# Two transformer-like acts on one core: no added room behind the reciprocals, and optional work of each act's first stage laid into its first phases

## The reference

```
x = x + squared_attention(norm(x))   # scores squared, causal, divided by their row sums, then @ Wo
x = x + gated_attention(norm(x))     # one key/value head, picked per token by an argmax gate; softmax
x = x + mqa_attention(norm(x))       # one key/value head, softmax, biases, then @ out_w
x = x + gated_attention(norm(x))     # the same weights as layer 2
```

## Time and profile before

| what | value |
|---|---|
| median of 3 runs | 4017.52 us (4014.93 to 4022.45) |
| the profiled execution's own time | 4020.66 us |
| its span in the profile | 4018.9 us |
| PE busy | 3647.1 us, 91% |
| POOL busy | 2982.7 us, 74% |
| DVE busy | 2170.1 us, 54% |
| ACT busy | 1624.3 us, 40% |
| mean granted clock of TensorE | 0.977 |
| first keys burst of the first act | at 94.77 us |
| first keys burst of its second stage | at 307.91 us |
| second act's first keys burst | at 1104.43 us |

### The profile page before, as it was taken

One profiled execution on the slowest core, in us unless ns is written; L12 is line 12 of the kernel. 1 busy time (PEld: TensorE's weight loads), 2 busy tenths in 40 slices (PEclk: granted clock), 3 DMA queues, 4 the chain that ended last, 5 costly groups with the idle time before them and its releaser, 6 DMA issues.

```text
span 4018.9 us, 66697 instructions
## 1 busy us (share of the span) xinstructions
PE 3647.1 (91%) x25570; PEld 1450.4 (36%) x25570; DVE 2170.1 (54%) x5132; ACT 1624.3 (40%) x2433; POOL 2982.7 (74%) x2207
## 2 busy tenths in 40 slices
PE   8899999997989999999888888888998999999976
PEld 5343534432333333333333333333333333333332
DVE  1222323233556766666666656565665666676663
ACT  1554545554043333434444434343332334343343
POOL 3988788896067767777888877787667677776786
PEclk9999999998999999999999999999999999999997
DMA  2000101020110010100101010010101001010011
GB/s 74 27 6 27 38 16 48 6 70 33 45 33 1 32 32 1 64 1 25 40 13 53 6 48 12 30 35 17 48 1 35 30 1 64 1 54 1 1 43 32
DMA packets 63286, 115.02 MB, mean 29 GB/s; under 512 B 8576, under 2 KB 9088, under 8 KB 62976
## 3 DMA queue, kind: packets, MB, share of 16 engines
q1 hardware_dynamic: 62976, 110.75, 8.5%
HBM read 77.17 MB, written 33.55 MB: 28 GB/s over the span
## 4 chain that ended last, share of the span: by engine, by line
PE 54%; DVE 7%; ACT 6%; issue 4%; POOL 3%; DMA 0%; POOLq 0%; SPq 0%; DVEq 0%; ACTq 0%
PE banks L1181 11%; PE banks L1134 11%; PE banks L1166 9%; PE banks L1228 8%; PE banks L1127 7%; ACT probs_soft L870 5%; PE banks L1163 3%; DVE banks L966 3%; PE banks L1327 3%; DVE maxima_soft L961 2%; POOL added_soft L781 2%; PE banks L1195 1%; DVE rest_soft L1085 1%; DVE maxima_soft L966 1%; PE banks L1325 0%
## 5 line engine op out<-in xcount | busy, mean ns | idle before, releaser
L870 ACT ACTIVATE probs_soft<-banks 128x1024 f32<-128x1024 f32 (+1 forms) x960 | 848.4, 936 | 1195.1 <-PE banks L1166 1171.2
L781 POOL TENSOR_TENSOR added_soft<-added_soft,probs_soft 128x512 f32<-128x512 f32 (+1 forms) x380 | 1153.0, 3034 | 21.3 <-POOL added_soft L774 6.4
L966 DVE CUSTOM_DVE_ANT_0 banks<-banks,mask 128x128 f32<-128x128 f32 (+3 forms) x1536 | 701.3, 528 | 516.5 <-PE banks L1181 516.0
L961 DVE TENSOR_REDUCE maxima_soft<-banks 128x2 f32<-128x1024 f32 x384 | 452.6, 1221 | 367.5 <-PE banks L1181 367.4
L1181 PE MATMUL banks<-k_soft,q_soft 32*128 32x512 f32 (+3 forms) x4608 | 499.7, 525 | 77.6 <-ACT probs_soft L870 77.4
L876 ACT ACTIVATE probs_squared<-banks,key_scale_squared 128x512 f32<-128x512 f32 (+3 forms) x768 | 379.7, 590 | 341.5 <-PE banks L1166 337.1
L1127 PE MATMUL banks<-xnT,wide 128*128 128x512 f32 x1024 | 509.9, 620 | 5.0 <-DVE rest_soft L1085 1.9
L1134 PE MATMUL banks<-wide,xnT 128*128 128x512 f32 x1024 | 497.0, 613 | 1.0 <-ACT q_soft L853 1.0
L1166 PE MATMUL banks<-q_soft,k_soft 32*128 32x512 f32 (+3 forms) x4608 | 476.0, 495 | 0.0
L758 POOL TENSOR_SCALAR_AFFINE_SELECT probs_soft<-probs_soft 128x512 f32<-128x512 f32 x384 | 239.4, 637 | 313.8 <-ACT probs_soft L870 308.3
L1228 PE MATMUL banks<-probs_soft,v_soft 128*32 128x512 f32 (+3 forms) x4608 | 438.3, 499 | 20.2 <-ACT q_soft L855 4.8
(11 more groups left out here) (136 smaller groups left out, 4075.7 us busy)
## 6 DMA issues: line engine op xcount, KB each, us to landing
tiles<-out SPq DMA_DIRECT2D x96, 256.0 KB, 2.7
rest_soft<-out SPq DMA_DIRECT2D x96, 256.0 KB, 2.9
out<-rest_soft SPq DMA_DIRECT2D x96, 256.0 KB, 2.1
tiles<-in_x SPq DMA_DIRECT2D x32, 256.0 KB, 2.7
rest_squared<-in_x SPq DMA_DIRECT2D x32, 256.0 KB, 2.8
out<-rest_squared SPq DMA_DIRECT2D x32, 256.0 KB, 2.0
wide<-in_gated_wqkvT SPq DMA_DIRECT2D x3, 1024.0 KB, 7.6
probs_squared<-in_squared_wk SPq DMA_DIRECT2D x1, 1024.0 KB, 5.5
```

Of the source, the lines that this page charges most:

```text
L781: ins = pool.tensor_tensor(sums, sums, slot(ph, n)[:, :, col:col + width], ALU.add)
L870: ins = act.activation(slot(ph, n)[:, 2 * a:2 * a + 2, 0:width], score_pair(e, a)[:, :, 0:width], ACT.Exp, scale=SCALE)
L961: ins = dve.reduce_max(m["maxima"][:, ph % 2, 2 * a:2 * a + 2, t, p], score_pair(e, a)[:, :, col:col + width], AX_X)
L966: ins = dve.tensor_tensor_reduce(scores, scores, k["mask"][:, CHUNK - width:CHUNK], 1.0, MASKED, ALU.add, ALU.max, m["maxima"][:, ph % 2, ...
```

## The change

It has three parts. First, the constant `INVERTED` is gone: the halves that hold a reciprocal (`inv`) no longer get 0.85 more room, so `spread` lays the same optional work of the second act out more evenly. Second, in the first act only the values of the first two head groups and the features (`k2`, `q2`, `ksq`, `kvar`) of group 0 stay in front of the first phase; the features of group 1 (`rest`) become a work list of their own, due 2 halves before the end of phase 0, and the values of the other two groups one that is due 4 halves into phase 2. `since` lets them come from the start. Third, in the second act the second chunk of group 1's queries moves from in front of the `rows` bursts to between them, both key transposes (`kt`) come behind its first chunk, and the last two of the 8 `vall` move from between the `rows` bursts into phase 0, due at its half 6.

```diff
-INVERTED = 0.85
@@ keys_and_values
+        if s == 0:
+            return [("gt", s, 0)], first + [("krep", s, 1), queries[1][0], ("kt", s, 0), ("kt", s, 1)], \
+                [queries[1][1]] + [("vall", s, t) for t in range(NT)]
         first += [queries[1][0], ("krep", s, 1), ("kt", s, 0), queries[1][1], ("kt", s, 1)]
@@ phase
         for event, later in sums_done(kinds[of // NG], of, c):
             at[first + later].append(event)
-            if event[0] == "inv":
-                room[first + later] += INVERTED
@@ since
+    if event[0] == "v2" and event[1] == 0 or event[0] in ("q2", "k2") and event[1] < NG:
+        return 0
@@ plan
-        events += between + first
+        values = [e for e in between + first if e[0] == "v2"]
+        events += [e for e in values if e[2] == 0] + [e for e in first if e[0] != "v2"]
+        behind_first = [(in_pieces(rest, kinds), HALVES - 2), (in_pieces([e for e in values if e[2]], kinds), 2 * HALVES + 4)]
     if soft:
         rows = [("rows", 0, k) for k in range(NRB)]
+        behind_first = [(in_pieces(rest[len(rows) - 2:], kinds), 6)]
+        rest = rest[:len(rows) - 2]
...
-    else:
-        events += rest
...
+        if s == 0:
+            work = work[:1] + behind_first + work[1:]
```

## The result

| | before | after |
|---|---|---|
| median of the runs that were compared | 4018.23 us (4014.93 to 4022.45) | 3956.92 us (3951.94 to 3962.06) |
| ratio, 95% interval | | 0.9847 [0.983, 0.9864] |
| the profiled execution's own time | 4020.66 us | 3959.07 us |
| its span | 4018.9 us | 3957.3 us |

The kernel is 61 us (1.5%) faster.

The account below looks back on a forecast made before the run. PE, busy 91% of the span, bounds the kernel; only its idle time and slow stretches can be won. -18.0 - 2.0 - 10.0 + 2.5 (more rows in PE's list) = -27.5, from the median 4017.52 to 3990 us, range 3968 to 4010.

Parts of the forecast that it names:

- Part 1: First act's start: work moved behind the first keys burst fills PE's idle and slow time, 18.0 us gained.
- The sum's idle part: First act's first phases: 20.5 us of PE idle time goes, less 5 for POOL and 1.3 behind ACT's first squaring.
- The sum's clock part: First act's first phases: about 5.1 us of slow matmuls goes, less 1.3 of slow clock behind remaining waits.
- Part 2: Second act's start: 7.3 us of moved work goes to a stretch with idle time, 2 us gained, bounds -3 and 7.
- Part 3: Second act, no added room behind the reciprocals: net 10 us gained, bounds 25 gained and 45 lost.
- (a): Second act, sixth keys burst: a piece fills PE's 1.03 us wait for masked maxima in 14 of 27 phases, 13 us gained.
- (b): Second act: fewer outputs queue behind DVE's reciprocals, so a quarter of PE's 37 us of bank waits goes, 9 us.
- (c): Second act, bursts behind the reciprocals: PE arrives sooner and waits more for unmasked maxima, 12 us lost.
- Levelling wins more: Rival, chance 0.17: even pieces in the second act also shrink the 159 short waits for the exponential; 3968 us.
- POOL keeps the start: Rival, chance 0.14: first act's removed waits return in phases 1 and 2, gaining only 10 there; 4009 us.
- reciprocals decide: Rival, chance 0.06: in 43 second-act phases a keys burst waits for maxima behind DVE's reciprocals, 44 us lost; 4044 us.
- Slow clock from chopping: Rival, chance 0.03: moved matmuls between short waits run at half clock, costing 29.5 us more; about 4020 us.

Follow-up runs that it names:

- the changed kernel: The kernel before with only the second act's start changed: 4023.75 us, ratio 1.001.
- a step of 0.2 or 0.4 below zero: Room behind reciprocals 0.2 below zero, on the kernel before with only the first act's start changed: 4003.74 us; 0.4 below zero, on the kernel after: 4010.62 us.
- 0.85, 0.4, 0 and -0.2: Added room behind the reciprocals, on the kernel before with only the first act's start changed: 4006.23, 3942.63, 3954.99 and 4003.74 us.

## Why the prediction was off, step by step

**Part 1, the first act's start: the waits were right, the clock was not.** Predicted 18 us, measured 13.7 alone [8.8 to 18.5]. The start of PE in the kernel after:

```profile
64.95 1.14 PE L1171 MATMUL banks<-q_squared,k_squared 32*128 32x512 f32 x8
66.03 5.42 PE L1132 MATMUL banks<-xnT,wide 128*128 128x512 f32 x12
...
175.56 1.99 PE L1293 MATMUL banks<-wide,xnT 128*128 128x256 f32 x8 [1.13 <-ACT sums_squared L860]
...
188.67 1.71 PE L1233 MATMUL banks<-probs_squared,v_squared 128*32 128x512 f32 x16 [2.78 <-POOL probs_squared L763]
```

The keys burst stands at 64.95 (predicted 65.3). Of the two waits of the earlier trace rows the one of 5.48 us for the squares is gone, and the 9.57 us have become 2.78 (predicted 5). The product behind it takes 1.71 instead of 3.21 us, so the clock held there. The 1.3 us behind ACT's late first squaring didn't come: PE goes on at 66.03 without a wait. POOL in the kernel after, against the earlier trace rows:

```profile
72.58 0.64 POOL L763 TENSOR_SCALAR_AFFINE_SELECT probs_squared<-probs_squared 128x512 f32<-128x512 f32 x1 [2.53 <-ACT probs_squared L881]
...
187.88 0.64 POOL L763 TENSOR_SCALAR_AFFINE_SELECT probs_squared<-probs_squared 128x512 f32<-128x512 f32 x1
```

Its first mask stands at 72.58 (predicted 72.8), the mask that releases the product ends at 188.52, 8 us behind the earliest time of 180.6 that the working gave. POOL does pause where PE's list grew longer, as it said; but PE comes to that product at 185.9 and not at 178, so that only 2.78 us of it showed.

The sum's idle part, 20.5 less 5 and 1.3, is 14.2 us, and PE's idle time in this stage did fall by 14.2 (23.0 to 8.8). That the two agree to the tenth is luck: the wait for POOL is smaller than taken, and small waits for ACT and DVE at the moved pieces (1.13 us for a bank that ACT takes out, for one) make up for it. The sum's clock part, 5.1 less 1.3, is 3.8 us. This is the term that failed: PE is busy for 219.6 us, and 190.1 plus the 29.8 us that moved in are 219.9, so 0.3 us came. The slow stretches of the earlier trace rows are gone, and two others have come, around the variance matmuls and behind waits for ACT of 0.28 and 1.32 us:

```profile
133.00:141.00 8.00, 7.72 (x33) 4.10 (x31) 0.35 (x2) 2.77 (x8) 7.90 (x8) 0.79 0.01 2
253.00:262.00 9.00, 7.68 (x31) 3.88 (x30) 0.35 (x2) 3.00 (x5) 8.92 (x6) 0.81 0.00 1
```

**Part 2, the second act's start: small, as said, but not a gain.** Predicted 2 us gained with bounds from -3 to 7; measured 4 [0 to 8] lost alone, 2 to 4 lost in company. The wait stayed between 1 and 4 us, as said (3.08 us, against 1.91 before). The step that failed is the 2 us itself, that the moved work would meet idle time in stage 0. PE's idle time there is 15.7 us with and without it, and PE's busy time grew by 9.5 us for 7.3 us of work. The clock behind the first keys burst isn't the difference, though the rows of the changed kernel look like it. The kernel before, behind the earlier trace rows:

```profile
1104.65 1.04 PE L1166 MATMUL banks<-q_soft,k_soft 32*128 32x512 f32 x8
1105.62 2.01 PE L1127 MATMUL banks<-xnT,wide 128*128 128x512 f32 x2
1107.56 1.89 PE L1181 MATMUL banks<-k_soft,q_soft 32*128 32x128 f32 x16
```

Its keys burst is fast, and the two rows behind it take 0.9 and 0.7 us too long, where in the changed kernel it is the burst (1.96 us for 1.04) and the row behind it (2.59 for 1.98). So the kernel before pays about the same for its one wait, one row later. Of the 2.6 us by which the burst came less early than work was taken away, 1.2 are the longer wait; the rest wasn't traced.

**Part 3, no added room: the direction was right and the size wrong, by a factor of five.** Its three terms:

(a) Predicted: the waits of about 1 us at the sixth keys burst halve, 13 us. Right: in the second act 26 waits of 1.03 us for masked maxima are now 13. All waits for masked maxima went from 57.6 to 39.7 us.

(b) Predicted: "DVE takes outputs out behind its reciprocals", so a quarter of 37 us, 9 us, goes. This step failed, in its cause and in its size. The wait was the right one (a bank that DVE frees late), but the reciprocal is the smaller part of what stands ahead. The earlier trace rows gave me 924 ns, and the wait in the earlier trace rows is 3.39 us: a wait of more than three such instructions could not be one reciprocal. DVE's timeline, which I didn't read there, has the answer: maxima of 2.4 to 2.7 us, a reciprocal, then the addition. Shortening the reciprocals took the distance in stages 5 to 8 from 40 to 31 us, shortening the maxima from 40 to 6. Over the whole kernel the waits for these additions fell from 53.9 us (six rows, of which the 37 us were three) to 34.1, by 20 us; outside stages 5 to 8 they did not fall.

(c) Predicted: 12 us of new waits for unmasked maxima. They went from 22.4 to 29.7 us.

Two terms stood at nothing. The waits for ACT's exponentials, of which the forecast said that most of their neighbours stay as they are, fell by 20 us (77.4 to 56.9). And the clock: with only the room removed, PE's busy time fell by 14.6 us. The waits of that kernel, less those of the kernel before, give 16 for (a), 20 for (b), 19 for ACT and 7 lost for (c), together 49; 7 us of other waits came in, which leaves the 41.5 us of idle time, and 14.6 of clock make the 56 us between these two profiled executions.

Why I didn't see it: the earlier trace rows sums 43 phases into one, so that it didn't show that all ten waits at L1327 and all four at L1127 stand in stages 5 to 8; and I took the clock of 0.99 over 2564 us for "no effect", where the phase of stage 7 had 0.94. The prediction also left a half out: the reciprocals stand in halves 11 to 14 and 17 to 19 of a phase, and half 19 holds two of them and had twice the added room.

**The rivals.** "Levelling wins more" (3968) came nearest, and its sign did show: the waits for ACT fell from 187 to 122 times, 77.4 to 56.9 us, as much as the waits for outputs. Yet in stages 5 to 8, where two thirds of the gain lie, these give 5.7 of 40 us. "POOL keeps the start" and "reciprocals decide" did not come: the second stage starts at 293.4, and the reciprocals' length is worth nothing in the kernel after. "Slow clock from chopping" I gave 0.03, by the mean clock of 0.99. It was wrong for the change, and yet I dismissed too much: the *kernel before* paid it, where several waits of 2 us stood in one phase (0.94 in the phase of stage 7, 1.90 us against 1.03 for the same burst). In that phase the clock is 0.98 with only the room removed, 0.99 with only the reciprocals shortened and 1.00 in the kernel after. The Trainium skill ("TensorE: Matmul & The Clock Gate", "A second HAM failure mode: psum-queue depth-cycling") tells of a kernel that cycles through PSUM banks and idles so often for a short time between groups of matmuls that the clock swings. The trace agrees only in part: some 300 short waits leave 0.99 over 2564 us, and in the phase of stage 7 the clock falls behind single waits of 1.94, 1.99 and 2.92 us.

The criterion that I set for a wrong forecast, a change of the second act's length by over 25 us, was met: it fell by 41.3.

**What stays open.** Why a step of 0.2 or 0.4 below zero costs about 50 us. The traces show in which stages (5 to 8 above all: 32 of 47 us for the step of 0.2, 36 of 47 for that of 0.4), that ACT waits longer for the gate, and that the clock is lower, but no run isolates one of them. The share of the clock in part 3 is read from busy time, and no run sets it by itself. That the output's place and not that of the other pieces is what costs 21 us in stages 5 to 8 is read from the waits; no run moves the outputs alone.

## What to carry to other kernels

When a wait for another engine is longer than the instruction you blame, read that engine's timeline just ahead of the release: here it held 2.7 us of maxima, 0.9 of reciprocal and 0.6 of the addition itself. What a piece of work costs by its place is the whole queue ahead of the instruction that frees its bank, so count all of it. Sum such waits by stage, not over the whole kernel, since an order that is bad in four of twelve stages looks like noise in the total, and look at the clock of single phases too. A knob that shifts where a planner lays its pieces has no slope that can be trusted: of 0.85, 0.4, 0 and -0.2 the two ends took over 60 us more than the best, so try several values, and choose by stage.

## What the runs showed of the hardware that I had not expected

- The clock falls after fairly short waits. After 1.50 and 1.58 us, with a rows burst between, the keys burst took 1.96 us and four matmuls 2.59 (1.04 and 1.98 elsewhere for the like). A single wait did it too: after 1.91 us at 1104.43 of the kernel before, the two rows behind the next burst took 2.01 and 1.89 us (1.12 and 1.15 elsewhere). Yet the kernel before has 26 waits of 1.03 us for masked maxima, and its clock from 1230.7 to 3794.5 us was 0.99.
- Engines' queues couple more than their busy shares tell. DVE was busy for 616 of 1033 us in stages 5 to 8, and reducing this to 337 us took 55 us off the kernel before in these stages (1032.6 to 977.7), although PE was the engine with the most work throughout.
- The cost of more rows in PE's list, priced at 2.5 us for 28, can't be seen: PE's busy time fell by 8.2 us.
